# Two reorderings in the drain of a tokenizer stage: VectorE's bias parts behind the third norm, TensorE's last tokenizer product behind the scan's first output product

## The reference

```python
# tokenizer: per 4x4 patch, one query (the patch mean) attends to its 16 pixels
q  = ln(reduce_feats) @ Wq.T ; k, v = ln(pixels) @ Wkv.T
h  = reduce_feats + softmax(q*scale . k) @ v @ proj_w.T + proj_b
# scan layer on norm(h), 256 tokens an image taken in sequences
x_proj = xn @ Wx + bx ; Bm, C = split(xn @ Wbc + bbc) ; delta = xn @ Wd + bd
A_bar  = exp(-softplus(delta)) ; u = (1 - A_bar) * Bm * x_proj
s_t    = A_bar_t * s_(t-1) + u_t          # associative scan
h      = h + (C * s) @ Wy + by
# tree feed-forward on norm(h): 8 levels, sign of (x . w1[node] + b1[node]) picks the child
h      = h + sum over the 8 nodes of a path: gelu(|score|) * (x @ w2[node] + b2[node])
```

## Time and profile before

| What | Value |
|---|---|
| median of three runs | 612.56 us (611.96 to 614.68) |
| the profiled execution | 610.55 us, of which the span is 608.8 us |
| TensorE busy (matmul) | 570.6 us, 94% of the span |
| VectorE busy | 527.1 us, 87% |
| ScalarE busy | 462.8 us, 76% |
| GpSimd busy | 453.2 us, 74% |
| granted TensorE clock, mean | 0.983 |
| first block ends, second begins | 324.07 us (end of the last L1035), 324.53 us (first L1839) |

### The profile page before, as it was taken

The page is one execution under the profiler, slowest core; times in us unless marked ns, Lnnn a source line. Parts: engine busy times, 40 slices in busy tenths (PEclk is TensorE's granted clock), DMA queues, the critical chain, the costliest instruction groups (busy, mean ns, idle before and its releaser), DMA issues. The chain is left out here.

```text
span 608.8 us, 16030 instructions
## 1 busy us (share of the span) xinstructions
PE 570.6 (94%) x5276; PEld 299.5 (49%) x5276; DVE 527.1 (87%) x1029; ACT 462.8 (76%) x968; POOL 453.2 (74%) x458
## 2 busy tenths in 40 slices
PE   6899999999999999999769999999869999999995
PEld 4222333232223333232235666666537888888884
DVE  3589999999999999999984899999988888888883
ACT  3898888888888888887355888888656777777772
POOL 6856998989988998876575157777777767667676
PEclk9999999999999999999999999999988999999998
DMA  7333333322233332100002994111123333322200
GB/s 266 160 136 140 140 139 139 135 73 86 125 139 139 139 139 86 66 11 2 15 0 83 233 210 109 50 45 40 40 70 108 82 83 85 77 70 73 70 18 1
DMA packets 49602, 58.19 MB, mean 96 GB/s; under 512 B 31932, under 2 KB 44836, under 8 KB 47544
## 3 DMA queue, kind: packets, MB, share of 16 engines
q1 hardware_dynamic: 44120, 49.23, 26.9%
q0 software_dynamic: 5120, 6.99, 3.5%
q10 hardware_dynamic: 288, 1.05, 0.4%
HBM read 50.19 MB, written 10.28 MB: 99 GB/s over the span
## 5 line engine op out<-in xcount | busy, mean ns | idle before, releaser
L872 PE MATMUL s_proj<-x_px,w_kv 64*64 64x512 f32 x256 | 129.4, 604 | 2.1 <-DVE qk L643 1.3
L876 PE MATMUL s_proj<-x_px,w_kv 64*64 64x512 f32 x256 | 130.5, 609 | 0.0
L2203 POOL DMA_INDIRECT out<-orow,m_rows x96 | 94.0, 979 | 41.1 <-issue 35.4
L1317 POOL DMA_INDIRECT rows_by_group<-r_pay,r_slot_i x64 | 73.5, 1148 | 32.3 <-DVE r_slot_i L1640 9.9
L528 POOL TENSOR_TENSOR half_px<-x_px 128x1024 f32<-128x1024 f32 x30 | 71.3, 2378 | 28.0 <-DMA x_px<-in_x 28.0
L549 POOL TENSOR_TENSOR pre<-va 128x1024 f32<-128x1024 f32 x32 | 76.2, 2381 | 21.2 <-DVE va L659 19.3
L643 DVE TENSOR_TENSOR qk<-s_proj,q 128x512 f32<-128x512 f32 x128 | 86.5, 677 | 3.8 <-ACT q L375 1.9
L659 DVE TENSOR_TENSOR va<-b_a,v_sb 128x1024 f32<-128x1024 f32 x62 | 75.6, 1220 | 5.4 <-PE b_a L906 5.3
L2172 PE MATMUL s_delta<-m_xsT,m_w_cur 128*64 128x128 f32 x1152 | 71.1, 273 | 0.0
L320 ACT ACTIVATE x_sq<-x_px 128x1024 f32<-128x1024 f32 x64 | 67.5, 1055 | 4.1 <-PE b_x L943 4.1
L903 PE MATMUL b_a<-a_sb,e_sw 64*64 64x512 f32 x124 | 63.9, 596 | 5.4 <-DVE va L659 3.5
(11 more groups left out here) (333 smaller groups left out, 1750.5 us busy)
## 6 DMA issues: line engine op xcount, KB each, us to landing
x_px<-in_x SPq DMA_DIRECT2D x15, 2048.0 KB, 7.8
m_rows<-rows_by_group SPq DMA_DIRECT2D x96, 72.0 KB
wt<-in_w2T SPq DMA_DIRECT2D x8, 512.0 KB
rows_by_group<-rows_by_group SPq DMA_DIRECT2D x1, 2286.0 KB, 9.7
out<-orow,m_rows POOLq DMA_INDIRECT x96, 2.3
x_px<-in_x ACTq DMA_DIRECT2D x2, 512.0 KB, 6.0
x_px<-in_x SPq DMA_DIRECT2D x2, 512.0 KB, 7.1
rows_by_group<-r_pay,r_slot_i POOLq DMA_INDIRECT x64
```

Source lines behind the costliest of these rows:

```text
L872: mm(b_k[i][HI, :], w_kv[LO, 0, :], px(t, j, LO), start=True, stop=True)
L876: mm(b_k[i][LO, :], w_kv[HI, 0, :], px(t, j, HI), start=True, stop=True).then_inc(done["kv_product"], 1)
L1317: g.indirect_dma_start(rows_d, bass.IndirectOffsetOnAxis(ap=slot_i[:, c % 2, k:k + 1], axis=0), pay[:, c % 2, k, :], None).then_inc(scatte ...
L2203: nc.gpsimd.indirect_dma_start(out_d, bass.IndirectOffsetOnAxis(ap=rows[:, i, ID0:ID0 + 1].bitcast(I32), axis=0), orow[:, i, :], None, bou ...
```

## The change

`bias_parts()` moves on VectorE from step 17, ahead of the four `va_mul` of tile 15, to step 18, behind the norm of scan tile 2, where only the last `finish` follows it in the block. `out_mm(15)` moves on TensorE from step 19, ahead of `residual_first` and the third `delta_first`, to behind both. Nothing is added or taken away; the number of instructions of each engine stays.

```diff
             if t == TILES + 1:
                 delta_limit()
                 normalise_first(0)
-                bias_parts()
             pool_last(t)
...
                 normalise_first(1)
                 scan_first()
                 normalise_first(2)
+                bias_parts()
...
             spread(t - 3, 3)
-            if t > LAST_EARLY + 4 and t != TILES + 2:
+            if LAST_EARLY + 4 < t < TILES + 2:
                 out_mm(t - 4)
...
         residual_first()
         delta_first(2)
+        out_mm(TILES - 1)
         inputs_second()
```

## The result

The changed kernel takes 607.82 us (median of 17 runs, 604.98 to 611.62), the kernel before 611.96 us beside it (17 runs, 608.81 to 614.96). The ratio of the means is 0.9938, with a 95% interval of 0.9917 to 0.9958: 3.8 us faster, 2.6 to 5.1. The prediction was 609.2 from a median of 612.56, so 3.4 us faster; 607.82 lies in its range. The time of a run goes with the granted clock averaged over it: of the 17 runs of the changed kernel the five longest (609.03 to 611.62 us) had 0.981 to 0.984, the other twelve 0.985 to 0.990.

A forecast was written before the change was run, and what follows sets the result against it. TensorE was taken to set the first block's barrier, through waits for VectorE and GpSimd. 1.6 - 0.6 + 1.84 - 0.5 + 1.1 gives 3.4 us, so 609.2 from 612.56; range 607.0 to 611.8.

The forecast's parts named there:

- Bias parts off their place: First block's drain: moving 4.83 us of VectorE work removes TensorE's wait at the third spread piece, gaining 1.62 us.
- Scans beside GpSimd: Two VectorE scans in the drain: GpSimd's folds hold both, 2.9 us in place of 2.31, costing 0.6.
- Costs at nothing: End of the drain: last tokenizer product finds its fold done; bias parts take 1.9 us, VectorE ends at 320.1.
- The output product no longer behind: TensorE in the drain: the scan's output product starts at 317.0, right behind the gated output, gaining 1.84 us.
- The level in the tail: TensorE's clock from the output product to block end: leaned to 1.00, 3.4 us earlier; at 0.50, 1.7 earlier.
- signs of being wrong: Bias parts over 4 us; clock 0.50 in the tail; or first L1839 as early as predicted, span end not moved.
- The clock at 301: Rival: TensorE's clock doesn't fall at 301, third spread piece up to 1.6 us sooner; gain 4.2 to 5.0; chance 0.22.
- the case that was forecast: The drain with the clock's fall at 301 and level 1.00 in the tail: 3.4 us faster, 609.2; chance 0.36.
- the rival of 1.7 us: Rival: the clock falls again in the drain's tail, gain only 1.7 us, 610.9; chance 0.26.

The follow-up runs named there:

- the change again: The same full change, run and profiled once more against the kernel before: 606.99 us against 612.14, ratio 0.9919; drain 24.49 us, span 603.5.

## Why the prediction was right, and where it was not

The drain between the two fixed points, cut into stretches, with what the prediction's steps make of each (us):

| Stretch | Before | Predicted | Changed, first profile | Changed, second | Bias parts alone |
|---|---|---|---|---|---|
| first fixed point to the start of the scans | 20.12 | 18.5 | 18.33 | 16.82 | 18.43 |
| the two scans | 2.31 | 2.9 | 2.91 | 2.58 | 2.90 |
| scans to the end of the gated output | 0.78 | 0.8 | 0.79 | 0.79 | 0.78 |
| gated output to the start of L1026 | 1.84 | 0.05 | 0.05 | 0.06 | 0.26 |
| L1026 to the end of the block | 4.29 | 3.7 | 5.38 | 3.78 | 3.20 |
| barrier | 0.46 | 0.46 | 0.46 | 0.46 | 0.46 |
| whole drain | 29.80 | 26.4 | 27.92 | 24.49 | 26.03 |

*Bias parts off their place: right.* The wait at the third spread piece is gone, TensorE ran on at once, and the bias parts alone bring all that the change brings (0.9934 against 0.9938). Of the 4.83 us of work that leave, most turn into waits for TensorE that VectorE did not have before: 1.72 us ahead of the first multiplication, 0.30 ahead of the second and 0.84 ahead of the third.

*Scans beside GpSimd: right in size and cause.* 2.9 us were predicted, 2.91 came, and 1.27 when GpSimd is held off. The first scan (312.54 to 314.07) ends 0.55 us behind L560, the second (to 315.45) 0.55 behind L570. That is less than the 0.68 of a scan without GpSimd, so by these rows the hold is nearly, but not quite, as long as the whole instruction.

*Costs at nothing: right.* Bias parts 1.97 us (1.9 predicted), the fold in time, VectorE's last instruction done at 320.62, ahead of TensorE's 321.67.

*The output product no longer behind: right for the whole change, wrong as the worth of its second part.* L1026 starts 0.05 us behind its data, as the sum has it. But the 1.84 us are not the second part's. The fold starts from the same multiplications that the first part moves earlier: it ends 2.3 us earlier, counted from the first fixed point (318.67 - 294.73 against 315.87 - 294.21), ahead of the gated output, which moves by less because the scans take longer. So with the bias parts alone L1026 is already only 0.26 us behind. The prediction's own figures held this: they put the end of the fold near 316.8 and that of the gated output at 316.95. Read as a sum of two parts, 1.62 - 0.6 gives 1.0 us for the bias parts alone, and 4.0 came in the timed runs (2.5 to 5.6). The drain of its profile is 3.77 us shorter: 1.69 for the wait, less 0.59 for the scans, 1.58 for L1026 and 1.09 for the same products at the full clock (3.20 us in place of 4.29). On top of the first part, the second gives nothing that can be measured.

*The level in the tail: not settled by the prediction, and where the size is in part luck.* A clock of 0.50 in the tail stands among its signs of being wrong, and the first profile shows it; there the second block starts at 322.13, not near 321.2. The second profile shows 1.00. The tails of 5.38 and 3.78 us are near what the prediction had for either level, 5.4 and 3.7.

*The clock at 301.* The first profile has the fall. In the second it came earlier and the scans start 1.5 us sooner, where that rival had up to 1.6. So neither profile of the changed kernel is the case that was forecast, with the fall at 301 and none in the tail: the first is the rival of 1.7 us (1.88 came), the second that of 4.2 to 5.0 (5.31 came). The timed gain of 3.8 us lies between them, and that it came out near 3.4 is in part luck. The profile of the bias parts alone has the clock levels of the forecast, and 3.77. By the two profiles of the changed kernel, 27.92 and 24.49 us, executions of one program differ here by nearly as much as the change is worth; how often each level occurs was not counted, so this part of the size stays open.

## What to carry to other kernels

Two waits that follow from one late instruction are one gain: before adding two, ask whether the second wait's releaser moves with the first. Reordering two instructions pays only when the operand that was waited for first is the later one, and here about as much as it is later, so decide it after the other changes, not before. The bias parts and the scans, VectorE work that only reads and writes SBUF, took 1.97 and 1.27 us with GpSimd idle, and 4.83 and 2.91 beside it: such work is worth a place where GpSimd is idle, and where both are on one path, try to hold back the one that has slack. And take more than one profile of a program before a stretch of 28 us is explained to the last us.

## What the runs showed that I had not expected

The hold works both ways: GpSimd's L579 takes 0.88 us beside a scan and 0.61 without (in the changed kernel and with the fold held). The same two scans took 1.27 us with GpSimd idle, 1.55 where only the end of a fold lay beside them, and 2.31, 2.58 or 2.91 beside several folds, by how their start fell among these. The bias parts, too, grow where a held fold runs beside them: 2.74 to 3.02 us in place of 1.97.

The length of a wait does not tell whether the clock falls: 1.79 us was followed by 0.51 (only the product moved), 2.01 and 2.07 by none (only the bias parts; the change again), 2.40 by 0.50. With eight small products in the wait the one profile shows 1.00, which the changed kernel's second profile has without them; whether they help was not settled.
